# A selective-scan block and a routed mixture of experts on one core: products moved to GpSimd, a longer ring of state tiles, and filler products on TensorE

## The reference, cut to what matters

```python
xi = in_proj_w @ ctx                        # per sequence: 256 channels x 256 steps
u = silu(causal_conv4(xi) + conv_b)
dt_lo, Bm, Cm = split(x_proj_w @ u)         # 8, 16 and 16 rows
delta = softplus(dt_proj_w @ dt_lo + dt_proj_b)
def step(state, (d_t, B_t, C_t, u_t)):      # state: channels x 16
    state = state * exp(d_t * A) + (d_t * u_t) * B_t
    return state, (state * C_t).sum(over the 16 states)
y = (scan(step) + D * u) * silu(layernorm(x).T)
x = x + tanh(g_xattn) * y.T
h = layernorm(x)
top2 = top_k(h @ gate_w, 2)
x = x + tanh(g_ffn) * sum_e weight_e * ((silu(h @ w0[e]) * (h @ w1[e])) @ wo[e])
```

## Time and profile before

| what | us |
|---|---|
| median of 3 runs (297.35 to 299.65) | 299.03 |
| the profiled execution | 299.81 |
| its span, first to last instruction | 298.0 |
| scan stage, first scan to end of the last | 26.55 to 146.28 |
| last GpSimd product with C ends | 146.56 |
| first product of the first expert starts | 173.25 |
| mean granted TensorE clock, share of 2.4 GHz | 0.956 |

### The profile page before, as it was taken

One profiled execution on the slowest core, in us unless ns is written; L12 is line 12 of the kernel. 1 busy time (PEld: TensorE's weight loads), 2 busy tenths in 40 slices (PEclk: granted clock), 3 DMA queues, 4 the chain that ended last, 5 costly groups with the idle time before them and its releaser, 6 DMA issues.

```text
span 298.0 us, 4632 instructions
## 1 busy us (share of the span) xinstructions
PE 264.1 (89%) x1158; PEld 178.3 (60%) x1159; DVE 231.5 (78%) x406; ACT 185.1 (62%) x343; POOL 175.4 (59%) x159
## 2 busy tenths in 40 slices
PE   7985696999889898978989899999999999999970
PEld 7432342343335352523576667989898989898850
DVE  2989999999999999999859539888665656565630
ACT  2895759766685658778488215565657575756540
POOL 6103288999999998999500321546564656465242
PEclk9999799999999999999978669999999999999996
DMA  7699300000000001000198401242333333343322
GB/s 237 211 390 387 143 2 0 1 0 0 0 1 2 1 0 70 0 0 3 45 347 278 142 21 34 38 69 41 67 45 63 51 57 53 53 55 51 36 25 31
DMA packets 16678, 22.74 MB, mean 76 GB/s; under 512 B 2570, under 2 KB 10290, under 8 KB 16658
## 3 DMA queue, kind: packets, MB, share of 16 engines
q1 hardware_dynamic: 11472, 16.41, 15.7%
q0 software_dynamic: 4416, 6.03, 12.9%
q10 hardware_dynamic: 770, 0.06, 0.2%
HBM read 17.38 MB, written 5.11 MB: 75 GB/s over the span
## 4 chain that ended last, share of the span: by engine, by line
PE 62%; DVE 15%; issue 11%; POOL 6%; ACT 3%; POOLq 1%; DVEq 0%; ACTq 0%
PE PD L1046 11%; PE PZ L1086 11%; PE PU L1046 10%; PE PY L860 7%; DVE states L1255 5%; POOL hC L421 5%; PE PY L1072 4%; DVE states L1261 3%; PE PZ L1037 2%; PE PZ L921 2%; PE PY L855 1%; PE PU L768 1%; PE PD L805 1%; PE PY L1029 1%; PE PU L846 1%
## 5 line engine op out<-in xcount | busy, mean ns | idle before, releaser
L421 POOL TENSOR_TENSOR hC<-states,WO 128x512 f32<-128x512 f32 x63 | 79.9, 1280 | 15.1 <-PE PY L860 10.1
L1261 DVE TENSOR_TENSOR_SCAN states<-PD,states 128x512 f32<-128x512 f32 x64 | 77.6, 1214 | 1.1 <-ACT PD L629 0.9
L860 PE MATMUL PY<-hC,ident 128*128 128x512 f32 x128 | 67.5, 610 | 4.1 <-POOL hC L421 4.0
L456 POOL DMA_INDIRECT out<-lg,y_at x23 | 37.2, 1618 | 49.1 <-ACT lg L734 41.2
L629 ACT ACTIVATE PD<-WO,Aneg 128x510 f32<-128x510 f32 x64 | 43.9, 689 | 18.6 <-DVE states L1261 15.5
L442 POOL DMA_INDIRECT hC<-x_rows,x_at x23 | 27.2, 1183 | 33.7 <-DMA x_rows<-u 19.5
L1255 DVE TENSOR_TENSOR states<-PU,WO 128x512 f32<-128x512 f32 x64 | 42.9, 672 | 1.2 <-POOL hC L421 1.0
L718 ACT ACTIVATE hidT_hi<-PY 128x512 fp32r<-128x512 f32 x23 | 13.8, 600 | 38.7 <-PE PY L1072 38.7
L1510 DVE TENSOR_TENSOR WO_lo<-WO,WO_hi 128x512 fp32r<-128x512 f32 x46 | 29.7, 688 | 6.1 <-issue 5.7
L860 PEld LDWEIGHTS PY<-hC,ident 128*128 128x128 f32 x128 | 22.5, 191 | 16.6 <-POOL hC L421 11.2
L1498 DVE TENSOR_TENSOR dA<-PU,dA 128x512 f32<-128x512 f32 x23 | 15.9, 691 | 21.1 <-PE PU L1046 21.1
(11 more groups left out here) (238 smaller groups left out, 513.1 us busy)
## 6 DMA issues: line engine op xcount, KB each, us to landing
W<-in_L_ffn_w SPq DMA_DIRECT2D x16, 512.0 KB, 10.5
WO<-in_L_ffn_wo SPq DMA_DIRECT2D x8, 512.0 KB, 6.2
xs<-in_x SPq DMA_DIRECT2D x2, 512.0 KB, 5.5
out<-xs SPq DMA_DIRECT2D x2, 512.0 KB, 3.1
early<-in_ctx SPq DMA_DIRECT2D x1, 512.0 KB, 4.3
x_rows<-u SPq DMA_DIRECT2D x1, 512.0 KB, 6.0
x_rows<-u SPq DMA_DIRECT2D x2, 256.0 KB, 2.7
hC<-x_rows,x_at POOLq DMA_INDIRECT x23
```

Of the source, the lines that this page charges most:

```text
L421: pool.tensor_tensor(hC[:, n % 2, :], states[:, n % RING, :], C_rep[:, pair % C_RING, :], ALU.mult).then_inc(hc_done, 1)
L456: pool.indirect_dma_start(out=out, out_offset=bass.IndirectOffsetOnAxis(ap=y_at[:, s:s + 1], axis=0), in_=y_tile[s % 2], in_offset=None, c ...
L860: pe.matmul(PY[:, h, :], ident[:, :], hC[:, n % 2, :], start=False, stop=(m == DS - 1)).then_inc(y_done, 1)
L1261: dve.tensor_tensor_scan(states[:, n % RING, :], DEC[n % 2], states[:, n % RING, :], 0.0, ALU.mult, ALU.add).then_inc(scan_done, 1)
```

## The change

1. For the five pairs 5, 11, 17, 23 and 28 (`POOL_PAIRS`) GpSimd makes the product of B and delta u (`times_B`) instead of VectorE's `drive`. ScalarE copies the B row from PSUM into one SBUF tile `B_rep`, which GpSimd reads (`copy_B`, ahead of the decay of tile 2p-1). GpSimd does tile n+4 right behind its product with C of tile n. TensorE's `spread_C` behind such a pair waits for the copy instead of the drives.
2. The product with C is done in place in the state tile. `hC` goes, the ring of state tiles has six places instead of four, and a place is free again when TensorE has summed it (`y_done`) instead of when GpSimd has used it.
3. GpSimd makes 12 lower parts in the scan (`LOWER_AT`) instead of 18; six others come in the expert rounds 0 to 5, one each, behind the gather. VectorE makes 14, as before. `SPLITS` and the waits of gate and up are reordered to suit.
4. Behind the scan the spins go, and `fill` products take their place: fp32r 128x512 each, 3 ahead of the router, 3 ahead of the ranks, 17 behind them, one between each four products of both tables (3 + 3), 6 between the tables and 3 behind the first `x_turn`. The gated rows of x2 are made half by half between the two halves of the router.

```diff
-LATE = tuple(range(EARLY, EARLY + 8)) + (28, 29, 26, 27, 30, 31)
-GATE_LOW, UP_LOW = {3: 2, 4: 4, 5: 6, 6: 8, 7: 12}, {6: 10, 7: 14}
-SPINS = (4, 1, 2)
+LOWER_AT = (4, 9, 12, 15, 21, 24, 26, 34, 37, 40, 46, 49)
+LATE_DVE, LATE_POOL = (18, 19, 12, 13, 20, 21, 14, 15, 22, 23, 24, 25, 26, 27), (16, 17, 28, 29, 30, 31)
+GATE_LOW, UP_LOW = {3: 2, 4: 6, 5: 10, 6: 12, 7: 14}, {3: 4, 4: 8}
+UP_LOW_POOL = {5: 2, 6: 4, 7: 6}
+POOL_PAIRS = (5, 11, 17, 23, 28)
+FILL = {"gated": 3, "mask": 3, "places": 17, "rows": 1, "weights": 6, "table": 1, "turn": 3}
-RING = 4
+RING = 6
...
+            def times_B(n):
+                q, pair, h = n // (2 * DS), n // 2, n % 2
+                pool.wait_ge(b_copied, POOL_PAIRS.index(pair) + 1)
+                pool.wait_ge(du_pool if q else du_ok, h + 1)
+                pool.wait_ge(y_done, n - RING + 1)
+                pool.tensor_tensor(states[:, n % RING, :], B_rep[:, :], du[2 * q + h], ALU.mult).then_inc(dbu_pool, 1)
...
-                    if n >= 2:
-                        pool.wait_ge(y_done, n - 1)
-                    pool.tensor_tensor(hC[:, n % 2, :], states[:, n % RING, :], C_rep[:, pair % C_RING, :], ALU.mult).then_inc(hc_done, 1)
-                    if n in SPLIT_AT:
-                        lower(SPLIT_AT.index(n))
+                    pool.tensor_tensor(states[:, n % RING, :], states[:, n % RING, :], C_rep[:, pair % C_RING, :], ALU.mult).then_inc(hc_done, 1)
+                    if (n + 4) // 2 in POOL_PAIRS:
+                        times_B(n + 4)
+                    if n in LOWER_AT:
+                        lower(LOWER_AT.index(n))
...
+                if s < len(LATE_POOL):
+                    lower(LATE_POOL[s])
...
+            def copy_B(pair):
+                act.wait_ge(b_ps, pair + 1)
+                if POOL_PAIRS.index(pair):
+                    act.wait_ge(dbu_pool, 2 * POOL_PAIRS.index(pair))
+                act.activation(B_rep[:, :], BCR[pair % 2], ACT.Copy).then_inc(b_copied, 1)
...
+                    if h == 1 and pair + 1 in POOL_PAIRS:
+                        copy_B(pair + 1)
...
+            def fill(place, to):
+                for _ in range(FILL[place]):
+                    pe.matmul(to, W1_hi[:, 0, 0, 0:P], W1_hi[:, 0, 0, :], start=True, stop=True)
...
+            fill("gated", TABLE)
             router(1, 0)
+            pe.wait_ge(base_kept, 2)
+            gated_rows(0, 0)
             router(1, 1)
+            gated_rows(1, 0)
+            gated_rows(0, 1)
+            gated_rows(1, 1)
+            fill("mask", TABLE)
             ranks()
+            fill("places", TABLE)
...
                 if n >= RING:
-                    dve.wait_ge(hc_done, n - RING + 1)
+                    dve.wait_ge(y_done, n - RING + 1)
...
-                    if n + 1 < NT:
+                    if n + 1 < NT and (n + 1) // 2 not in POOL_PAIRS:
                         drive(n + 1)
```

More of the change, by code:

```diff
@@ L51 @@
 UNROLL = 6
-SPLITS = tuple((w, e, k) for w, experts in ((1, range(6)), (0, range(E)), (1, range(6, E))) for e in experts for k in range(2))
+SPLITS = tuple((w, e, k) for w, experts in ((1, range(3)), (0, range(3)), (1, range(3, 6)), (0, range(3, E)), (1, range(6, E)))
+               for e in experts for k in range(2))
 SPLIT_AT = (3, 6, 9, 12, 15, 18, 24, 26, 31, 33, 36, 39, 41, 44, 47, 49, 52, 54)
@@ L127, in build @@
         z_cols = zs.rearrange("p t (l r) -> p t r l", r=2)
+        B_rep = sb("B_rep", [P, QT])
         ident = sb("ident", [P, P])
@@ L198, in overlay @@
             return nc.alloc_sbuf_tensor_at(name, shape, F32R, offset=offset)
-        x_tile = [hC[:, 0, i * DX:(i + 1) * DX] for i in range(2)]
+        x_tile = [states[:, 4, i * DX:(i + 1) * DX] for i in range(2)]
         row_hot = overlay("row_hot", [P, NQ * TOPK * QBLK, P], at_states)
@@ L283, in build, with by_dve @@
         block = stack.enter_context(nc.Block())
+        def by_dve(pairs):
+            return 2 * sum(p not in POOL_PAIRS for p in range(pairs))
         def whole_part(i):
@@ L919, in add_gz @@
                     for h in range(2):
-                        alone = q == 1 and r == 0
-                        mm = pe.matmul(x2[:, l, h, :], z_cols[:, q * QBLK + 2 * r + h, l, :], scaled_id[:, :],
-                                       start=alone, stop=(alone or (l == 1 and h == 1)))
+                        mm = pe.matmul(x2[:, l, h, :], z_cols[:, q * QBLK + 2 * r + h, l, :], scaled_id[:, :], start=False, stop=(l == 1 and h == 1))
                 mm.then_inc(x2_ps, 1)
@@ L997, in _, with gated_rows @@
             through(ADD_NEXT_AT + 1, NT)
[L999 to L1002 removed]
+            def fill(place, to):
+                for _ in range(FILL[place]):
+                    pe.matmul(to, W1_hi[:, 0, 0, 0:P], W1_hi[:, 0, 0, :], start=True, stop=True)
+            def gated_rows(r, h):
+                pe.wait_ge(gz_ok, 2 + h + 1)
+                x2 = PZ[r][:, :].rearrange("p (l e h) -> p l h e", l=2, h=2)
+                for l in range(2):
+                    mm = pe.matmul(x2[:, l, h, :], z_cols[:, QBLK + 2 * r + h, l, :], scaled_id[:, :],
+                                   start=(r == 0), stop=(r == 0 or (h == 1 and l == 1)))
+                if h:
+                    mm.then_inc(x2_ps, 1)
             pe.wait_ge(scan_done, NT)
             pe.wait_ge(W_hi_ok, 1)
+            pe.wait_ge(dbu_done, by_dve(NT // 2))
+            pe.wait_ge(c_ok, NT // 2)
+            fill("gated", TABLE)
             router(1, 0)
+            pe.wait_ge(base_kept, 2)
+            gated_rows(0, 0)
             router(1, 1)
[L1008 to L1012, removed]
+            gated_rows(1, 0)
+            gated_rows(0, 1)
+            gated_rows(1, 1)
+            fill("mask", TABLE)
             ranks()
[L1014 to L1015 removed]
+            fill("places", TABLE)
+            pe.wait_ge(slot_id_ok, 1)
             pe.wait_ge(logits_ok, 2 * NQ)
[L1017 to L1019 removed]
             n = NQ * TOPK * QBLK
@@ L1022, in _ @@
                 if j % 4 == 0:
+                    if j:
+                        fill("rows", PD[1][:, :])
                     pe.wait_ge(row_hot_ok, j // 4 + 1)
@@ L1025, in _ @@
             mm.then_inc(table_ps, 1)
-            spin(SPINS[1])
+            fill("weights", PD[1][:, :])
             pe.wait_ge(slot_w_ok, 2)
             for j in range(n):
+                if j and j % 4 == 0:
+                    fill("table", PD[1][:, :])
                 mm = pe.matmul(bank[5][:, 0:2 * COLS].rearrange("p (i s) -> p i s", i=2), row_hot[:, j, :], slot_w[:, :, j, :], start=(j == 0), stop=(j == n - 1))
@@ L1102, in step @@
                 down(s, i)
-            spin(SPINS[2] // 2)
             x_turn(0, 0, 16)
-            spin(SPINS[2] - SPINS[2] // 2)
+            fill("turn", PD[1][:, :])
             pe.wait_ge(slots_ok, 1)
             first = expert_of(0)
-            pe.wait_ge(W_lo_pool, EARLY)
+            pe.wait_ge(W_lo_pool, len(LOWER_AT))
             pe.wait_ge(W_hi_ok, len(SPLITS))
@@ L1519, in _ @@
             split_x(1, 1)
-            lower(LATE[:2])
+            lower(LATE_DVE[:2])
             hidden(0, 0)
```

30 lines of the change are left out of this document (19 added, 11 removed).

## The result

The changed kernel takes 301.37 us, the median of 20 runs (299.66 to 305.19); the kernel before took 298.87 in 20 runs beside it (296.91 to 300.16). The ratio is 1.0084 (95% interval 1.0061 to 1.0106): 0.8% slower, inside the range and inside the 1% that was forecast as no change. The profiled execution took 300.83 us with a span of 299.0, 1.0 longer than before. Its terms are not those of the forecast: the three that the forecast added up are each larger, and cancel.

A forecast was written before the change was run, and what follows sets the result against it. The prediction took VectorE to bound the scan, with GpSimd close behind and next late, and TensorE a stretch of the experts. It summed 299.81 + 1.4 (GpSimd) - 1.3 (fills) + 0 (lower parts) = 299.9 us, range 295.0 to 303.5.

The forecast's parts named there:

- VectorE's drives: Scan: ten drives go, 6.0 us at most, plus 1.0 of waits; whether this reaches the end is up to GpSimd.
- GpSimd's sum: Scan: 107.0 us of work plus idle time, so GpSimd ends at 148.0 instead of 146.56, +1.4 us.
- The wait at pair 5: Scan, tile 10: GpSimd stands still about 3.3 us for ScalarE's copy of B ahead of the decay of tile 9.
- at pair 23: Scan: ScalarE's copy of B stands behind `x2_out`, so GpSimd loses 1.4 us behind the product of tile 42.
- the rest: Scan: GpSimd's other waits, behind copies of pairs 11, 17, 28 and late scans; 0 to 6 us, taken as 3.0.
- The rival on lateness: Scan: GpSimd's lateness reaches VectorE through TensorE's order; +4.4 at the upper end, 302.9 us in all, chance 0.18.
- the forecast's own case: Whole kernel: the likeliest case, 299.9 us, within 298 to 302, chance 0.46.
- The fills: Behind the scan: between -3.7 us if the clock holds and +1.0 if it falls again; the middle, -1.3, was taken.
- the better end: Behind the scan, clock holding: weight table -1.6, spins -1.9, first gate -0.9, fills inside the table +0.7; sum -3.7 us.
- The rival "the clock falls in spite of the fills": Behind the scan: TensorE's clock falls again, +1.0 us there, 302.2 us in all, chance 0.12.
- The six late lower parts: Expert rounds: they fit between GpSimd's gather and scatter, taken as 0; collisions with VectorE allowed 0 to +1.9 us.
- the prediction's own sign of being wrong: Expert rounds: longer than before, with VectorE's lower parts well over 0.69 us.

The follow-up runs named there:

- the early copy: Changed kernel, with ScalarE copying the B row right behind the decay of the tile before, ahead of the softplus and `x2_out`: 300.67 us, ratio 1.0060.
- the last run: Changed kernel with no pairs on GpSimd, late lower parts behind VectorE's WO parts, no fills: 298.81 us, against 295.19 with the fills.

## Why the prediction was right in the total and where its steps failed

**VectorE's drives.** Right that the saving wouldn't arrive: 6.0 us less of drives, 8.2 us of waits for the decay.

**GpSimd's sum** was right within 1.8 us. It counted 107.0 us of work and 13.1 of idle time (5.0 + 0.4 + 3.3 + 1.4 + 3.0) in 120.1. From 28.36 to 149.74 there are 121.4, and 13.0 are idle (7.7 + 5.9, less the 0.7 ahead of the first product). The wait at pair 5 was 2.98 for 3.3, at pair 23 2.43 for 1.4; the start took 6.1 for 5.4, and the rest 1.5 for 3.0. The later end, +3.2 instead of +1.4, is 0.4 of a later start and 1.4 of work.

**What it means for the scan** is the step that failed: "Whether this reaches the end of the scan is up to GpSimd". GpSimd's sum of work isn't what sets it: with four of the five pairs it has 85 of the 87 instructions, and the scan takes 118.09; with three it had room (17.3 us of idle time ahead of the products with C instead of 7.7), and the scan ended no earlier. The runs show two losses. The first the prediction had: the late copies at pairs 5 and 23. Without tiles 33 to 38 the scan takes 111.5 us in the changed kernel, 107.9 with the copies early and 110.0 in the kernel before. In this loss the clock has a share that isn't measured, as it fell to 0.58 at 50 to 54, behind the wait at pair 5, and didn't with the early copy. The second the prediction did not have: pair 17. It stands where the sequences change, with 16 products of 8 columns in TensorE's order, and GpSimd's two products in a row kept TensorE waiting there. With the clock at 1.00, as in the changed kernel's own profiled execution, tiles 33 to 38 take 10.99 instead of 9.76; where the clock falls they take 14.3, with five pairs or three and with the early copy or the late one. Without that pair it is 9.76 again. So its price is 1.2 us, or 4.6 where the clock falls. Why the clock falls there in one execution and holds in another of the same scan stays open, and leaving out pair 17 alone with the late copies was not tried. The prediction looked for falls of the clock behind the scan only.

**The rival on lateness** named the right place: the waits of the scans are for ScalarE's decay, behind spreads that stand behind late sums, and they shrink when the spreads get a tile more. Its price, +4.4, lies between the two lengths that this scan had in profiled executions, +2.7 and +6.7 over the 119.73 of before. That it stayed with 0.18 was too little; it happened together with the forecast's own case, and the fills paid for it.

**The fills** were taken at -1.3 between -3.7 and +1.0, and the passage gave -4.86, beyond the better end. The middle between two ends was no estimate: either the clock holds or it doesn't, and with the fills it held (1.00 against 0.52 in the last run). Then the terms of the better end came out. The weight table took 2.66 (169.44 to 172.10) instead of 3.61, -0.95 for the forecast's -1.6 + 0.7; from there to the first gate it was 1.05 instead of 3.03, -2.0 for -1.9. The first gate was mis-sized: the 2.27 of the earlier trace rows begin at 174.24, but the gate had begun at 173.25, and from the first gate to the second it went from 4.85 to 3.26, -1.6 for -0.9. The last 0.3 came ahead of the weight table. The dip that was expected behind 162 came at 156 to 159 and not again. The runs give 3.7 us to the fills; with neither fills nor spins the passage is 31.06, so that leaving out the spins and the new order of x2 account for some 0.8 (31.82 - 31.06). The rival "the clock falls in spite of the fills" is excluded for the tables of the changed kernel's profiled execution (1.00 from 165 to 175), but not for every execution: in that of the run with no pairs, with the same fills, the clock was 0.50 there.

**The six late lower parts** were taken at 0, at most +1.9; they cost 2.87. The step that failed is "its idle time covers it, and for two that it doesn't"; the prediction's own sign of being wrong, longer rounds with VectorE's lower parts well over 0.69, came true. The parts don't meet VectorE's by chance: the gather that GpSimd does ahead of them and the WO parts come at the same place of every round, and all six met. The WO lower parts together took 9.0 us longer (38.7 against 29.7), of which VectorE's idle time covered two thirds. The rule that the prediction quoted from the Trainium skill ("GPSIMD Engine Reference", section 8) spoke against the change and was right about the collisions. The Trainium skill says more in "SBUF — State Buffer", Terms: the pair of ports is locked for a whole instruction, and the engine that loses stands still. The trace agrees that a whole instruction is lost: 1.28 for the two parts and 1.30 for GpSimd's product make 2.58, and they took 2.62 to 3.00.

**The sum** was near because +2.7 and +0.4 in the scan, -4.9 behind it and +2.9 in the experts cancel as +1.4, -1.3 and 0 did. That they cancel is luck. The median of 20 runs is 1.5 above the forecast and 0.5 above the profiled execution, which has the short scan; that some of the others have the long one is likely, but not shown.

The best version is the ring of six and the fills with no product of B on GpSimd and the late lower parts behind WO (295.19, ratio 0.9866), or with pairs 11, 23 and 28 and the early copy besides (294.91, 0.9879). With four runs of each the two can't be told apart, and the first is simpler.

## What to carry to other kernels

When work is moved to an engine that has room in the mean, ask at each place what stands behind it in the next engine's order: with the copies early, the pairs of products on GpSimd cost the profiled executions nothing at four places and 4.6 us at a fifth, where they kept TensorE waiting ahead of narrow products and its clock fell. When a mend seems to give nothing, look at each stretch by itself: the early copies gave 3.5 us and the total hid it, because a fall of the clock elsewhere took 3.3. Two instructions that use the same port meet in every round if the same event lets both start, so that idle time in the mean covers little; one wait that puts the second behind the first gave 9.0 us of busy time back. A term whose two ends are two states (the clock holds or falls) is forecast as two cases, not by its middle.

## What was not expected of the hardware

A fall of TensorE's clock can come in the middle of a stage that is bound by another engine, and it makes TensorE the bound: busy 8.00 of 8.00 us at 0.57, with VectorE down to 5.53 of 8. A short idle time isn't enough to tell: with four pairs TensorE was busy for 1.61 of the 4 us from 46 on and the clock stayed at 1.00, in the changed kernel it was 1.78 of 4 and the clock was 0.58 in the 4 us behind. Beside one GpSimd product of 1.29 to 1.31 us, VectorE's pairs of instructions with two SBUF operands lost 1.34 to 1.72 us, so at least the whole of it and not a share. GpSimd's product took no longer than alone, although the profile has VectorE's instruction starting first each time (187.97 against 188.22 in the round shown); as its spans on GpSimd are rough, which of the two came first stays open.
